# A second mixer with the keys stationary and its denominators gathered chunk by chunk, and a last norm shared between two engines

## The reference

```python
xn = layernorm(x)                                  # 1024 x 512
q, k, v = split(xn @ Wqkv)                         # the second mixer, 8 heads of 64
q, k = elu(q) + 1, elu(k) + 1
kv = einsum('hnd,hne->hde', k, v)                  # one 64 x 64 matrix for a head
z = 1 / (einsum('hnd,hd->hn', q, k.sum(tokens)) + 1e-6)
mix = (einsum('hnd,hde->hne', q, kv) * z) @ Wout + bout
g = xn                                             # graph attention, twice
for l in range(2):
    g = batchnorm(g + edge_attention(g) @ Wo[l].T + bo[l])
    g = batchnorm(g + relu(g @ W1[l].T + b1[l]) @ W2[l].T + b2[l])
x = x + layernorm(g) * ln_g + ln_b + mix
y = layernorm(x)                                   # the last norm, without weights
out = x + y                                        # and 2.0 added at two columns of 80 to 112
# which columns: from y[:, 0:4] and y[:, 16:80] > 0.5 by way of a small network
```

## Time and profile before

| | us |
|---|---|
| median of 3 runs (lowest, highest) | 1181.24 (1179.94, 1181.41) |
| the profiled execution's own time | 1181.42 |
| its span, first to last instruction | 1179.7 |
| PE busy in the span | 1076.4 (91%) |
| DVE busy | 642.7 (54%) |
| ACT busy | 410.5 (35%) |
| POOL busy | 177.5 (15%) |

### The profile page before, as it was taken

The page is one execution under the profiler, slowest core; times in us unless marked ns, Lnnn a source line. Parts: engine busy times, 40 slices in busy tenths (PEclk is TensorE's granted clock), DMA queues, the critical chain, the costliest instruction groups (busy, mean ns, idle before and its releaser), DMA issues.

```text
span 1179.7 us, 14861 instructions
## 1 busy us (share of the span) xinstructions
PE 1076.4 (91%) x5638; PEld 693.6 (59%) x5638; DVE 642.7 (54%) x1162; ACT 410.5 (35%) x560; POOL 177.5 (15%) x119
## 2 busy tenths in 40 slices
PE   6999999899878999989999999989899999999914
PEld 2726446687657867656666666434566666664413
DVE  5685666446684145246565664541455555654495
ACT  2401112354323122045454554110455555551004
POOL 2000000997144420000000000000000000003000
PEclk9999999899989999999999999999999999999967
DMA  8001000002000310200000020110000000100002
GB/s 313 36 0 36 36 18 1 1 1 72 1 1 1 108 36 1 72 1 1 1 1 1 1 73 1 35 37 36 1 1 1 1 1 1 37 1 19 1 0 72
DMA packets 17659, 31.08 MB, mean 26 GB/s; under 512 B 3708, under 2 KB 4924, under 8 KB 17342
## 3 DMA queue, kind: packets, MB, share of 16 engines
q1 hardware_dynamic: 14270, 28.08, 6.8%
q10 hardware_dynamic: 3328, 2.15, 0.6%
HBM read 28.12 MB, written 2.10 MB: 26 GB/s over the span
## 4 chain that ended last, share of the span: by engine, by line
PE 81%; DVE 10%; ACT 3%; issue 2%; POOL 2%; DMA 1%; DVEq 0%; SPq 0%; ACTq 0%; POOLq 0%
PE slots L1516 71%; PE slots L1583 11%; DVE PT L1343 1%; DVE KS L1333 1%; DMA W<-in_wkT 1%; POOL KR L583 1%; ACT KS L873 1%; POOL MASK L584 1%; DVE rstd L1207 0%; DVE SM L1397 0%; DVE X L1409 0%; DVE XT L1291 0%; DVE P0L L1172 0%; DVE st L945 0%; DVE st L1414 0%
## 5 line engine op out<-in xcount | busy, mean ns | idle before, releaser
L1516 PE MATMUL slots<-XT,W 128*128 128x512 f32 x320 | 143.0, 599 | 0.0
L1516 PE MATMUL slots<-KS,QS 64*128 64x512 f32 x768 | 108.6, 416 | 18.3 <-DVE KS L1333 9.9
L1516 PE MATMUL slots<-PT,XN 128*64 128x256 f32 x1024 | 117.6, 382 | 0.0
L971 DVE COPY PT<-slots 128x1024 f32<-128x1024 f32 x64 | 78.2, 1222 | 71.1 <-PE slots L1583 70.1
L645 POOL TENSOR_TENSOR QS<-QF,QS 128x512 fp32r<-128x512 f32 x16 | 20.6, 1287 | 555.0 <-PE slots L1583 359.8
L1516 PEld LDWEIGHTS slots<-XT,W 128*128 128x128 f32 x320 | 59.1, 190 | 73.2 <-issue 71.5
L1516 PE MATMUL slots<-PT 128*128 128x512 bf16 (+3 forms) x408 | 96.9, 370 | 1.5 <-ACT PT L676 1.2
L1516 PEld LDWEIGHTS slots<-KS,QS 64*128 64x128 f32 x768 | 73.2, 190 | 39.9 <-issue 10.0
L1516 PEld LDWEIGHTS slots<-PT,XN 128*64 128x64 f32 x1024 | 70.7, 137 | 42.8 <-issue 9.8
L1343 DVE CUSTOM_DVE_ANT_0 PT<-slots,MASK 128x1024 f32<-128x1024 f32 x64 | 75.8, 1222 | 32.0 <-PE slots L1516 32.0
L1343 DVE CUSTOM_DVE_ANT_0 SM<-slots,MASK 128x1024 f32<-128x1024 f32 x64 | 75.8, 1222 | 30.5 <-PE slots L1516 30.5
(11 more groups left out here) (345 smaller groups left out, 1678.1 us busy)
## 6 DMA issues: line engine op xcount, KB each, us to landing
X<-in_x SPq DMA_DIRECT2D x4, 512.0 KB, 12.2
W<-in_wout SPq DMA_DIRECT2D x2, 1024.0 KB, 5.3
W<-in_gv SPq DMA_DIRECT2D x2, 1024.0 KB, 8.6
W<-in_gq SPq DMA_DIRECT2D x2, 1024.0 KB, 5.1
W<-in_gk SPq DMA_DIRECT2D x2, 1024.0 KB, 5.4
W<-in_go SPq DMA_DIRECT2D x2, 1024.0 KB, 6.6
W<-in_w SPq DMA_DIRECT2D x2, 1024.0 KB, 4.8
out<-X ACTq DMA_DIRECT2D x1, 1600.0 KB, 6.0
```

What stands on the lines that cost most here:

```text
L971: nc.vector.tensor_copy(dst, src).then_inc(dve_evacuated, 1)
L1516: return nc.tensor.matmul(o_, lhsT, rhs, start=start, stop=stop)
```

## The change

Three parts. **The mixer.** `kv1` now keeps the keys stationary and moves the values with two columns of ones behind each chunk's 128, so that product and key sums come out together (130 columns); the product then has the other orientation, and a new job `kvT1` turns it by four transposes. The denominators are taken for each chunk of the queries as soon as it is there: four jobs `den` 0 to 3 of 8 products each, with 128 tokens of the queries stationary and two columns of key sums moving; they lie among the `q1` jobs. What comes out has the tokens on the partitions, so the inverse is over a 128 x 64 tile, ScalarE and VectorE copy it out to full width (`zx`, two chunks each), and `zb` turns it by 8 transposes for each chunk. `gv0` 1 moves behind `zb`. ScalarE rounds the weight of `gv0` one place earlier, ahead of the last exponential of the queries. **The batch norm** behind the feed-forward block: VectorE applies chunk 0 alone, ScalarE chunks 1 and 2; the one behind the attention is as it was. **The last norm:** VectorE's sums into `X` give the row sums too (`accum_out`), and ScalarE takes mean and sum of squares of tiles 0 to 6; VectorE takes the statistics of tile 7. The comparison is made on `X` itself against a threshold, in one instruction with the weighting.

The diff, cut to its core (semaphore names, the new small tiles in `ag`, and `state`'s new counts are left out):

```diff
+AFTER_KEYS1 = [("kv1", 0), ("q1", 0), ("q1", 1), ("kvT1", 0), ("den", 0), ("q1", 2), ("den", 1), ("q1", 3), ("den", 2)]
...
-    add("kv1", 1, [V])
-    add("q1", 4, [V])
+    for job in AFTER_KEYS1:
+        jobs.append((job, V))
     add("mixM1", 2, [V])
-    add("den", 1, [V])
-    jobs.extend([(("gv0", 0), V), (("gv0", 1), A)])
-    add("zb", 4, [V])
-    jobs.extend([(("gv0", 2), V), (("gv0", 3), A)])
+    jobs.extend([(("den", 3), V), (("gv0", 0), V)])
+    add("zb", FC, [V])
+    jobs.extend([(("gv0", 1), A), (("gv0", 2), V), (("gv0", 3), A)])
...
+        V1 = PT[:, 4096:8256].rearrange("p (t c n) -> p t c n", t=TT, c=FC)
...
+            nc.gpsimd.memset(V1[:, :, :, P:P + 2], 1.0).then_inc(blk_made, 1)
...
             for j in range(4):
+                if j == 3:
+                    act.wait_ge(psum_full, INDEX[("q1", 3)] + 1)
+                    round_weight(3)
                 act.wait_ge(kneg, j + 5)
                 nc.scalar.activation(SM[:, j % 2, :], SM[:, j % 2, :], ACT.Exp).then_inc(kexp, 1)
-            act.wait_ge(psum_full, INDEX[("q1", 3)] + 1)
-            round_weight(3)
...
+            act.wait_ge(z_inverted, 1)
+            for c in (0, 2):
+                nc.scalar.activation(zx[:, c], z1[:, :, c, :].unsqueeze(3).broadcast_to([P, TT, 2, DH]), ACT.Copy).then_inc(z_spread_act, 1)
...
+                if j == 1:
+                    copy_out(GV[:, 2:4, :], "gv0", 1, lambda s: s.rearrange("p (t d) -> p t d", t=2))
...
+                def bn_chunk(n, c):
                     act.wait_ge(bn_ready, 2 * n + 1)
...
+                    nc.scalar.activation(XT[:, c, :], XT[:, c, :], ACT.Identity, bias=bns[:, 4 + c:5 + c],
+                                         scale=bns[:, c:c + 1]).then_inc(act_chunk_ready, 1)
...
+                take_std(4 * l + 3, 0, FC - 1)
+                bn_chunk(2 * l, 2)
+                take_std(4 * l + 4, FC - 1, FC)
...
+                take_std(4 * l + 5, 0, FC - 1)
+                bn_chunk(2 * l + 1, 1)
+                bn_chunk(2 * l + 1, 2)
+                take_std(4 * l + 6, FC - 1, FC)
+            take_std(3 + 4 * L, 0, TT // 2)
+            take_std(4 + 4 * L, TT // 2, TT)
+            for t in range(TT - 1):
+                act.wait_ge(y_summed, t + 1)
+                nc.scalar.activation(neg_mean[:, t:t + 1], ysum[:, t:t + 1], ACT.Copy, scale=-1.0 / D).then_inc(mean_taken, 1)
+                act.wait_ge(mean_taken, t + 1)
+                nc.scalar.activation(squares, X[:, t, :], ACT.Square, bias=neg_mean[:, t:t + 1], scale=1.0,
+                                     accum_out=ysq[:, t:t + 1]).then_inc(y_squared, 1)
+            take_std(5 + 4 * L)
...
+            kv4 = src.rearrange("p (c n) -> p c n", c=FC)
+            nc.vector.tensor_tensor(kvm, kv4[:, :, 0:P], blk4, ALU.mult)
+            nc.vector.tensor_tensor(KS1, kv4[:, :, P:P + 2], blk[:, ::DH].unsqueeze(1).broadcast_to([P, FC, 2]),
+                                    ALU.mult).then_inc(dve_evacuated, 1)
+            def denominators(c):
+                src = full(dve, "den", c)
+                nc.vector.tensor_scalar(z1[:, :, c, :], src[:, 0:2 * TT].rearrange("p (t e) -> p t e", e=2), 1e-6, None,
+                                        ALU.add).then_inc(dve_evacuated, 1)
+            for name, j in AFTER_KEYS1[1:]:
+                if name == "q1":
+                    elu1(QT1[:, j, :], "q1", j, 4 + j)
+                elif name == "den":
+                    denominators(j)
+                else:
+                    copy_out(kvT1, "kvT1", 0, lambda s: s[:, 0:D].rearrange("p (c n) -> p c n", c=FC))
...
+            denominators(3)
+            dve.wait_ge(*evacuated("den", 3))
+            nc.vector.reciprocal(z1.rearrange("p t c e -> p (t c e)"), z1.rearrange("p t c e -> p (t c e)")).then_inc(z_inverted, 1)
+            dve.wait_ge(z_inverted, 1)
+            for c in (1, 3):
+                nc.vector.tensor_copy(zx[:, c], z1[:, :, c, :].unsqueeze(3).broadcast_to([P, TT, 2, DH])).then_inc(z_spread_dve, 1)
...
-            for j in range(4):
+            for j in range(2):
                 dve.wait_ge(q1_scaled_rounded, j + 1)
                 nc.vector.tensor_tensor(Q1L[:, j, :], QT1[:, j, :], Q1R[:, j, :].bitcast(fp32), ALU.subtract).then_inc(q1_scaled_split, 1)
             copy_out(GV[:, 4:6, :], "gv0", 2, two)
+            for j in range(2, 4):
+                dve.wait_ge(q1_scaled_rounded, j + 1)
+                nc.vector.tensor_tensor(Q1L[:, j, :], QT1[:, j, :], Q1R[:, j, :].bitcast(fp32), ALU.subtract).then_inc(q1_scaled_split, 1)
...
-                    if c != FC - 2:
+                    if c in own:
...
+                branch_and_norm(f"wo{l}", f"gbo{l}", f"g1{l}", f"be1{l}", (0, 1, 3))
+                dve.wait_ge(act_chunk_ready, 3 * l + 1)
+                branch_and_norm(f"f{l}", f"gb2{l}", f"g2{l}", f"be2{l}", (0, 3))
...
+            for t in range(TT + 1):
+                if t < TT:
+                    src = full(dve, "gT", t // 2) if t % 2 == 0 else slot_of("gT", t // 2)
+                    step(("stats", t), nc.vector.bn_stats(st[:, t, :], two(src)[:, t % 2, :]))
+                if t >= 1:
+                    dve.wait_ge(dve_link, made["stats", t - 1])
+                    step(("moments", t - 1), nc.vector.bn_aggr(mv[:, t - 1, :], st[:, t - 1, :]))
+                if t == TT // 2 + 1:
+                    dve.wait_ge(dve_link, made["moments", TT // 2 - 1])
+                    var(TT // 2)
+            dve.wait_ge(dve_link, made["moments", TT - 1])
+            var(TT, TT // 2)
+            row_ready(dve, "L1_gnn_ln_g")
+            for n in range(TT + 1):
...
+                if n == 0:
+                    continue
+                if n == 1:
+                    inverse(TT)
+                    dve.wait_ge(shift_added, TT)
...
+                if t < TT - 1:
+                    nc.vector.scalar_tensor_tensor(X[:, t, :], SM[:, t % 2, 0:D], rstd[:, t:t + 1], X[:, t, :], ALU.mult, ALU.add,
+                                                   accum_out=ysum[:, t:t + 1]).then_inc(y_summed, 1)
+                else:
+                    nc.vector.scalar_tensor_tensor(X[:, t, :], SM[:, t % 2, 0:D], rstd[:, t:t + 1], X[:, t, :],
+                                                   ALU.mult, ALU.add).then_inc(y_summed, 1)
+            dve.wait_ge(y_summed, TT)
+            link(nc.vector.bn_stats(st[:, TT - 1, :], X[:, TT - 1, :]))
+            link(nc.vector.bn_aggr(mv[:, TT - 1, :], st[:, TT - 1, :]))
+            nc.vector.tensor_scalar(neg_mean[:, TT - 1:TT], mv[:, TT - 1, 0:1], -1.0, None, ALU.mult)
+            step("last_moments", nc.vector.tensor_scalar(rstd[:, TT - 1:TT], mv[:, TT - 1, 1:2], EPS, None, ALU.add))
+            dve.wait_ge(y_squared, TT - 1)
+            nc.vector.tensor_scalar(rstd[:, 0:TT - 1], ysq[:, 0:TT - 1], 1.0 / D, EPS, ALU.mult, ALU.add).then_inc(var_ready, 1)
+            rounds[0] += 1
+            dve.wait_ge(dve_link, made["last_moments"])
+            step("centred", nc.vector.tensor_tensor(XN[:, :, 0:4], X[:, :, 0:4],
+                                                    neg_mean.unsqueeze(2).broadcast_to([P, TT, 4]), ALU.add))
+            dve.wait_ge(i16_made, 2)
+            dve.wait_ge(std_ready, rounds[0])
+            step("threshold", nc.vector.scalar_tensor_tensor(half_up, rstd[:], 0.5, neg_mean, ALU.mult, ALU.subtract))
+            step("inverse", nc.vector.reciprocal(inv_std, rstd[:]))
+            dve.wait_ge(dve_link, made["threshold"])
...
+                last = nc.vector.scalar_tensor_tensor(bits[:, t], X[:, t, 16:80].rearrange("p (j n) -> p j n", j=4), half_up[:, t:t + 1],
+                                                      i16m.unsqueeze(1).broadcast_to([P, 4, 16]), ALU.is_gt, ALU.mult)
+            step("bits", last)
+            dve.wait_ge(dve_link, made["inverse"])
+            nc.vector.tensor_scalar(sumc[:, 0, :], inv_std, 1.0, None, ALU.add)
+            nc.vector.tensor_tensor(sumc[:, 1, :], neg_mean, inv_std, ALU.mult).then_inc(sum_ready, 1)
+            step("flag_cols", nc.vector.tensor_tensor(XN[:, :, 0:4], XN[:, :, 0:4],
+                                                      inv_std.unsqueeze(2).broadcast_to([P, TT, 4]), ALU.mult))
+            dve.wait_ge(dve_link, made["flag_cols"])
...
+            def denominators(slot, c):
+                need("kv1", 0)
+                need("q1", c)
                 for t in range(TT):
...
+                    last = mm(slot[:, 2 * t:2 * t + 2], QT1[:, c, t * P:(t + 1) * P], KS1[:, c, :], True, True)
+                return last
...
+            for name, j in AFTER_KEYS1:
+                slot = begin(name, j)
+                if name == "kv1":
+                    for c in range(FC):
+                        for t in range(TT):
+                            last = mm(slot[:, 256 * c:256 * c + P + 2], K1[:, t, c * P:(c + 1) * P], V1[:, t, c, :], t == 0, t == TT - 1)
+                elif name == "kvT1":
+                    need("kv1", 0)
```

(13 more changed lines are left out.)

142 lines of the change are left out of this document (40 added, 102 removed).

## The result

| | before | after |
|---|---|---|
| median of the runs (four of each) | 1180.76 us | 1163.89 us (1162.89 to 1167.77) |
| ratio, 95% interval | | 0.9863 (0.9844 to 0.9881) |
| the profiled execution, and its span | 1181.42, 1179.7 us | 1162.89, 1161.2 us |
| mean granted clock of that span | 0.973 | 0.978 |

The forecast was 1165.4 us, between 1163.0 and 1168.6. The change gives 16.9 us by the medians, 16.2 by the ratio (14.1 to 18.4 by its interval) and 18.5 by the two spans; the sum said 15.8.

What follows compares the result with a forecast made beforehand. TensorE's own work was taken to bound the mixer, VectorE's chain the end. 9.55 + 0.3 + 0.76 + 5.3 - 0.1 = 15.8 us off a span of 1179.7 gave 1165.4 us for the execution, range 1163.0 to 1168.6.

Steps and rivals of the forecast that it cites:

- What bounds the kernel: Whole kernel: TensorE's own work bounds the second mixer; at the end it waits 28.2 us for VectorE's features.
- The mixer: TensorE in the second mixer: kv1 6.8, den 0.35, zb 2.85 us less, kvT1 0.45 more; 9.55 us less in all.
- What must stay hidden: Mixer: gv0's weight, the last exponential, and zb's inputs could come late; all were taken as hidden behind TensorE's work.
- Step (a): Mixer, gv0's weight: rounded by about 436.3, TensorE there at 436.6, fits by 0.3 us; the old order would wait 2 us.
- a new wait in the mixer: Rival, mixer: if the two orders meet badly, TensorE waits up to ScalarE's 1.89 us, giving 1167.3 us; chance 8%.
- Batch norm: Behind the feed-forward blocks: chunk 3 starts 0.76 us sooner, worth 0.3 us in layer 0 and 0.76 in layer 1.
- The last norm: VectorE's chain at the end: 1.45 us a tile, comparisons 0.2 each, the minimum 5.3 us sooner.
- The tail: Behind the features: ScalarE's sums and store end just when TensorE's transposes do, taken as 0.1 us more.
- odd width: Rival, mixer: 130 columns or a two-column product cost 0.02 us more a record, 2.6 us, giving 1168.0; chance 6%.
- loss by the clock in the mixer: Rival: TensorE's clock falls at six places of barely streaming records, 16.5 us lost, giving 1181.9; chance 3%.
- rival on the tail's clock: Rival, tail: TensorE at full rate from the start, 16 transposes take 1.8 us less, giving 1163.6; chance 8%.
- the forecast as worked out: Whole kernel: the summed terms hold without any rival, 1165.4 us, own range 1164.3 to 1166.5; chance 61%.

Runs made afterwards that it cites:

- The parts measured alone: Three kernels, each the kernel before with one part of the change: mixer 0.9912, last norm 0.9958, batch norm 0.9982.
- weight_late: The changed kernel with ScalarE rounding gv0's weight behind the last exponential again, as before the change: 0.9896 of the kernel before, median 1172.7 us.
- the norm alone: The kernel before with only the last norm's part of the change: 0.9958 of the kernel before, 5.0 us less.
- warm_tail: The changed kernel with 68 transposes of the identity on TensorE ahead of the features, from the fourth sum on: 0.9869 of the kernel before, 1167.06 us.
- the last kernel: The changed kernel with four buffers, 68 identity transposes, ScalarE copying fT's second half before its last two output sums, first store later: 0.9833 of the kernel before, 1162.31 us.
- the two kernels with the late weight: The changed kernel with gv0's weight rounded late, with two columns in den (0.9896, 1172.7 us) or 64 (0.9916, 1172.0 us).

## Why the prediction was right, step by step

**What bounds the kernel.** Right: TensorE's own work in the mixer, VectorE's chain in the last norm. The parts measured alone add up to the whole within their intervals.

**The mixer** was forecast at 9.55 us and gave 10.33, in three traces within 0.02. By starts: `kv1` 7.14 for 14.28 us, so 7.14 less against 6.8; a record with 130 columns in one run of 64 is 0.112 us, and the 0.116 that I scaled came from runs of 16 between the small products. Why those were dearer is not shown; `q1` too starts slower behind a small product, its first record taking 0.31 to 0.33 us for 0.23. `den` 6.81 for 6.95, with the wait of 0.32 ahead of it gone: 0.46 against 0.35. `zb` 3.41 for 6.46: 3.05 against 2.85. Here I had misread: 7.18 us is the duration of the 64 transposes with the tail of the last. From their start at 195.07 to the next row of that timeline, shown below, it is 6.94 us, 0.108 each and not 0.112. `kvT1` 0.43 more against 0.45. The rest, 0.1 us, lies in `q1`, which starts anew behind each `den` and takes 22.16 for 21.89, and in `gv0` (22.01 for 22.32) and `mixM1` (3.52 for 3.60), which go the other way. What I left out was small and mostly on one side.

```profile
202.01 0.48 PE L1516 MATMUL slots<-X0R,Q0R 128*128 128x512 f32 x1
```

**What must stay hidden** stayed hidden. Step (a) was the tight one, with 0.15 us left for 0.3, and weight_late confirmed its arithmetic, a wait of 1.96 for 2. What such a wait can cost was too low in the text, and with it the rival "a new wait in the mixer": 1.89 us there; 4.6 in the trace in which the clock fell, 2.2 in the one in which it stayed.

**Batch norm.** 0.3 us in layer 0, forecast 0.3: chunk 3 came 0.71 us sooner against the coefficients, and TensorE's own records were the cap. In layer 1 0.71, forecast 0.76.

**The last norm.** 5.41 us from the first statistics of `gT` to the minimum (26.55 to 21.14; 5.49 from the last ones), forecast 5.3: tile 1.46 for 1.45, the accumulator's read at its lower bound (0.07 for 0), comparisons 0.2 each as taken. The order of ScalarE and VectorE never crossed: ScalarE was through with a tile well inside VectorE's period. The Trainium skill ("VectorE: DVE Perf Modes", section "Two Vector instructions with no wait between them") says that an operation which also writes out its accumulator is two instructions. The traces agree for this kind of instruction, with a record of 0.08 us of its own behind each sum; what I had drawn from it, 0.6 us more, did not come.

**The tail.** Forecast 0.1 us more; it took 17.32 us from the minimum to the first reduction of yT for 17.08 before, and 16.77 in the norm alone. Traces with the same tail differ by 0.5 us, with the moment at which the clock comes up; the 0.1 is not tested by that.

**The rivals.** No odd width (0.112 us for 130 columns, 0.106 for two). No loss by the clock in the mixer: it read 1.00 throughout. The rival on the tail's clock did not come about: `fT` took 3.68 us as before. Made to come about, it did not give its 1.8 us: at full rate from the start the tail loses or gains by what it then waits for, 0.7 to 1.25 us slower in warm_tail, 1.6 to 2.15 faster in the last kernel.

**The sum.** 15.8 us forecast; 16.9 by the first medians, and 10.33 + 0.30 + 0.71 + 5.41 = 16.75 by the pieces. The other 1.8 us between the two spans are clock and the first load (8.52 for 9.00 us) in code that no edit touches, less what the tail lost. The median, 1163.89 us, is 1.5 us below the forecast, 0.4 outside the narrow range of 1164.3 to 1166.5 that I had given the forecast as worked out, and nearest by number to the rival on the tail's clock, which is not what happened. About 0.9 us of the 1.5 lies in terms that were sized too small, 0.8 in the mixer (`kv1` 0.3, `zb` 0.2, `den` 0.1 and what was left out) and 0.1 in the last norm; the rest is within what executions of one kernel differ by.

Open: whether the late start of `kv1` in the traces of the two kernels with the late weight is more than what executions differ by, whether the medians of these two hold a fall of the clock more often than the traces show, and whether small records ahead of a wait make a fall of the clock likelier.

## What to carry to other kernels

Price a small product by its records, not its columns: an extra column in a product that is already there is nearly free, a separate one costs nearly as much as a full one (here 0.107 us for 8 columns, 0.116 for 128). Price a wait ahead of dense TensorE work by the wait and by the clock that it may take with it; where an engine is made faster in front of a wait, move what it waits for as well. Compare traces by distances between marks around the edit: two executions of one kernel differ by more than several of the terms here.
